# Eight chained layers on one core: quantised weights turned by DMA, feed-forward halves joined, half of attention's queries prepared by GpSimd

## The reference, cut to what matters

```python
x = x + L0_xattn(ln(x), token_ids, ctx, ctx, ctx)   # four experts of 256, silu; a mask by token picks one
x = x + L0_ffn(ln(x), w1, w3, w2)                   # hidden 682, w = clip(round(w/mean|w|), -1, 1) * mean|w|
x = x + L1_wkv(ln(x), ctx, w, u)                    # a recurrence over 256 steps
x = x + L1_moe(ln(x), ...)                          # shared ffn of 352, then 8 fused experts
x = x + L2_attention(ln(x), ctx, ...)               # 16 heads of 16; q, k, v and the probabilities rounded to 8 bits
x = x + L2_ffn(ln(x), w1, w2, w3)                   # hidden 704, w = clip(round(w/mean|w|), -1, 1), sigmoid gate
x = x + L3_linear_attention(ln(x), ctx, ...)
x = x + L3_ffn(ln(x), gate_w, up_w, down_w)         # hidden 1024; x, weights and hidden rounded in blocks of 32 (MX fp8)
```

## Time and profile before

| | us |
|---|---|
| median of 3 runs | 1064.69 (1057.3 to 1065.52) |
| profiled execution, its own time | 1067.97 |
| its span, first to last instruction | 1066.2 |
| PE, DVE, ACT, POOL busy | 874.2 (82%), 737.8 (69%), 459.8 (43%), 147.8 (14%) |
| TensorE clock granted, mean | 0.834 of full |
| chain that ended last | PE 51%, DVE 26%, ACT 9%, issue 7%, DMA 5% |

### The profile page before, as it was taken

How to read it: one execution, slowest core, us unless ns; L and a number is a source line. 1 busy time by engine, 2 the same in 40 slices (tenths; PEclk the granted TensorE clock), 3 DMA queues, 4 the chain that set the end, 5 groups by cost and what they waited for, 6 DMA issues and landing times.

```text
span 1066.2 us, 11685 instructions
## 1 busy us (share of the span) xinstructions
PE 874.2 (82%) x4250; PEld 517.8 (49%) x4250; DVE 737.8 (69%) x968; ACT 459.8 (43%) x694; POOL 147.8 (14%) x230
## 2 busy tenths in 40 slices
PE   5999884489799999988999567777788898878796
PEld 3444562244655555554555233434355566644555
DVE  2774558964457787788487987888864436659773
ACT  2213435642324422222223688989964435422110
POOL 1000000000013443236030111111101000001111
PEclk9999886579989999989999655555559979889898
DMA  8500002100122220330036799877760000000000
GB/s 268 175 0 1 1 0 44 23 3 6 21 44 44 40 36 12 67 51 0 1 45 113 146 152 162 150 138 127 139 93 30 1 0 1 1 0 1 10 10 20
DMA packets 206908, 57.96 MB, mean 54 GB/s; under 512 B 187694, under 2 KB 205188, under 8 KB 206852
## 3 DMA queue, kind: packets, MB, share of 16 engines
q1 hardware_dynamic: 206740, 57.05, 28.4%
q10 hardware_dynamic: 112, 0.17, 0.1%
HBM read 20.62 MB, written 1.05 MB: 20 GB/s over the span
## 4 chain that ended last, share of the span: by engine, by line
PE 51%; DVE 26%; ACT 9%; issue 7%; DMA 5%; POOL 1%; ACTq 1%; POOLq 0%; DVEq 0%
PE ps L900 47%; DMA arena<-xc 4%; DVE arena L2493 3%; ACT xc L1800 3%; ACT arena L1810 1%; PE ps L463 1%; DVE arena L2123 1%; PE ps L1030 1%; DVE xn_t L1940 1%; PE ps L1342 1%; DVE xc L2295 1%; ACT arena_split L1717 1%; DVE arena L2502 1%; DVE sq L2404 1%; DVE sq L2401 1%
## 5 line engine op out<-in xcount | busy, mean ns | idle before, releaser
L900 PE MATMUL ps<-arena 128*128 128x16 f16 (+7 forms) x1760 | 269.4, 324 | 66.5 <-ACT xc L1800 29.9
L900 PE MATMUL ps<-arena_split 128*128 128x512 f32 (+5 forms) x736 | 202.4, 439 | 27.5 <-DVE arena_split L1961 14.6
L900 PEld LDWEIGHTS ps<-arena 128*128 128x128 f16 (+4 forms) x1760 | 133.2, 130 | 177.6 <-issue 82.5
L900 PEld LDWEIGHTS ps<-arena_split 128*128 128x128 f32 (+5 forms) x736 | 136.0, 198 | 99.3 <-issue 39.5
L2493 DVE TENSOR_REDUCE arena<-ps 128x1 f32<-128x1024 f32 x128 | 152.4, 1220 | 28.1 <-PE ps L900 26.4
L1800 ACT ACTIVATE xc<-ps,arena 128x1024 int16<-128x1024 f32 x128 | 153.3, 1203 | 25.2 <-POOL arena L876 20.8
L900 PE MATMUL ps<-sq,arena 128*64 128x256 f32 (+3 forms) x256 | 80.9, 515 | 8.3 <-DVE sq L2404 8.3
L876 POOL TENSOR_SCALAR arena<-arena 128x1 f32<-128x1 f32 x128 | 33.9, 265 | 210.6 <-DVE arena L2493 210.6
L1584 ACT ACTIVATE act_buf<-ps 128x512 f32<-128x512 f32 (+2 forms) x34 | 20.3, 597 | 95.2 <-PE ps L900 95.1
L837 POOL TENSOR_SCALAR arena<-arena 128x512 f32<-128x512 f32 x12 | 23.0, 1921 | 248.3 <-DVE arena L2317 248.3
L900 PEld LDWEIGHTS ps<-sq,arena 128*64 128x64 f32 (+3 forms) x256 | 30.1, 166 | 43.6 <-issue 31.2
(11 more groups left out here) (287 smaller groups left out, 1328.5 us busy)
## 6 DMA issues: line engine op xcount, KB each, us to landing
arena<-in_L_ffn_w SPq DMA_DIRECT2D x4, 640.0 KB, 6.0
arena_split<-arena_split SPq DMA_DIRECT2D x59, 32.0 KB
arena<-xc SPq DMA_TRANSPOSE x96, 3.3
arena<-in_x SPq DMA_DIRECT2D x1, 1024.0 KB, 5.7
arena<-in_ctx SPq DMA_DIRECT2D x1, 1024.0 KB, 8.2
...
```

What stands on the lines that cost most here:

```text
L900: return pe.matmul(o, l, r, start=start, stop=stop)
```

## The change

Six things change. (1) DVE writes the ternary values of both `l0` and `l2` as bf16 into buffers of their own; SP issues the three DMA transposes of `l0` while `l0x` still runs, and ACT copies the result between units 13 and 14 of `l0x`; PE's transposes and GpSimd's casts are gone. (2) In every `ffn` the `down`s of the first half's last units are issued behind the first units of the second half, and `add_y` follows them (`summed`); `ln_steps` for six units becomes earlier in half 0 and later in half 1. (3) DVE makes only the scales of the second half's queries; multiply, rounding and copies are 24 pieces on GpSimd, one behind each of the first 24 row biases; the first half's four copies stand ahead of `xn`. (4) In the last layer the first three steps of `tokens_quantised` stand ahead of the norm's `xc`. (5) The second half of the tokens is quantised in one piece, of which GpSimd does the last three steps. (6) The last tile's gate, product, turn and copy run in two halves of 512 columns, GpSimd rounds the first one, and the last two tiles' `down` use banks 7 and 0.

```diff
-        def ln_steps(n):
+        def ln_steps(n, h):
             if n < 6:
                 return dict(mean=0, xc=0, sq=1, var=1, sd=2, diag=2, rows=2, xn=2, parts=2)
+            if n == 6 and h == 0:
+                return dict(mean=0, xc=0, sq=1, var=1, sd=2, diag=2, rows=3, xn=3, parts=4)
             if n == 6:
-                return dict(mean=1, xc=1, sq=2, var=2, sd=3, diag=3, rows=4, xn=5, parts=5)
+                return dict(mean=2, xc=2, sq=3, var=3, sd=4, diag=4, rows=5, xn=5, parts=5)
...
+            def ternary_turned(name, first):
+                for src, dst, at in zip(ternary_16[name], ternary_back[name], (first, first, first + 1)):
+                    sp.wait_ge(weights_fixed, at)
+                    sp.dma_start_transpose(dst.rearrange("p (a b) -> p a b", b=P), src).then_inc(load[name], 16)
+
+            ternary_turned("l0", 1)
...
+            ternary_turned("l2", 4)
+
             sp.wait_ge(bias_split, 2)
-            for src, dst in zip(ternary_16, ternary_back):
-                sp.dma_start_transpose(dst.rearrange("p (a b) -> p a b", b=P), src).then_inc(load["l2"], 16)
-
-            sp.wait_ge(bias_split, 3)
...
-            pool.wait_ge(weights_fixed, 2)
-            full = H2 // P
-            for w, o in zip(w_l2[0:2], ternary_16[0:2]):
-                o = o.rearrange("p (a b) -> p a b", b=D)
-                step(pool.tensor_copy(o[:, 0:full], w[:, 0:full]))
-                step(pool.tensor_copy(o[0:H2 % P, full], w[0:H2 % P, full]))
-                step(pool.memset(o[H2 % P:P, full], 0.0))
...
+            def late_query(u):
+
+                j, i = divmod(u, 6)
+                if j >= 4:
+                    return
+                if u == 0:
+                    pool.wait_ge(q_scaled, 1)
+                    pool.wait_ge(load["l2"], 16 * 8)
+                v = q_tok[:, 4 + j, :].rearrange("p (h d) -> p h d", d=HD)
+                o = q3[1][:, j]
+                if i == 0:
+                    inv = A["inv"][:, (4 + j) * HEADS:(5 + j) * HEADS]
+                    step(pool.tensor_tensor(v, v, inv.unsqueeze(2).to_broadcast([P, HEADS, HD]), ALU.mult))
+                elif i == 1:
+                    step(pool.tensor_scalar(o[:, :, 0, :], v, ROUND, ROUND, ALU.add, ALU.subtract))
+                else:
+                    n = HEADS // 4
+                    heads = slice(n * (i - 2), n * (i - 1))
+                    last = pool.tensor_copy(o[:, heads, 1:8, :], o[:, heads, 0:1, :].to_broadcast([P, n, 7, HD]))
+                    if i == 5:
+                        last.then_inc(q_split, 1)
...
+                late_query(u)
...
+            def rounded_by(v, power):
+                qf = power.rearrange("p (a b) -> p a b", b=MX_BLOCK)
+                step(pool.tensor_tensor(v, v, qf, ALU.add))
+                step(pool.tensor_tensor(v, v, qf, ALU.subtract))
+
             for t in range(TT):
-                v = h_tok[:, t % 2, :].rearrange("p (a b) -> p a b", b=MX_BLOCK)
+                half = 32 * (t % 2)
+                n = 32 if t < TT - 1 else 16
+                v = h_tok[:, t % 2, 0:n * MX_BLOCK].rearrange("p (a b) -> p a b", b=MX_BLOCK)
+                if t == 2:
+
+                    q = xn_tok[:, 4:8, :].rearrange("p t (a b) -> p (t a) b", b=MX_BLOCK)
+                    pool.wait_ge(xq_ready, 2)
+                    rounded_by(q, mxq[:, 4 * D:8 * D])
+                    back_scaled(q, mx_s[:, 0, 64:96], 32).then_inc(xq_ready, 1)
                 pool.wait_ge(mx_scaled, 24 + t + 1)
-                pool.tensor_tensor(v, v, mx_s[:, 0, 32 * (t % 2):32 * (t % 2) + 32].unsqueeze(2).to_broadcast([P, 32, MX_BLOCK]),
-                                   ALU.mult).then_inc(mx_fixed, 1)
+                if t == TT - 1:
+                    rounded_by(v, mxq[:, 0:n * MX_BLOCK])
+                back_scaled(v, mx_s[:, 0, half:half + n], n).then_inc(mx_fixed, 1)
...
-                        if i >= lag:
-                            down(i - lag)
+
+                        if h * s["n"] + i >= lag:
+                            down(*divmod(h * s["n"] + i - lag, s["n"]))
...
-            pe_turn(pe, "l0")
-            evacuated(pe, marks["l0"][1])
+            pe.wait_ge(weights_fixed, 3)
...
+                    j, c2_ = divmod(n, 2) if t < TT - 1 else (n % 2, n // 2)
...
+            down(TT - 2)
+            last_turned(0)
+            last_turned(1)
+            last_down(0)
+            last_down(1)
...
-            copy_out(act, "l0", False)
+            def ternary_copied(name, wts, h, i):
+
+                full, src, dst = h // P, ternary_back[name][i], wts[i]
+                act.wait_ge(load[name], 16 * 8)
...
+                    v = src.rearrange("p (r k j) -> p k r j", k=KC, j=P)
+                    act.activation(dst[:, :, 0:full * P].rearrange("p k (r j) -> p k r j", j=P), v[:, :, 0:full], ACT.Copy)
+                    act.activation(dst[:, :, full * P:], v[:, :, full, 0:h % P], ACT.Copy)
+
+            def first_ternary(i):
+                for part in {TERN_COPIED: (0, 1), TERN_COPIED + 1: (2,)}.get(i, ()):
+                    ternary_copied("l0", wt_l0, H0, part)
+
+            ffn(l0x, ACT.Silu, between=first_ternary)
             ffn(l0, ACT.Silu, tern_s[0][:, 8:9])
             passed = 0
...
+                def summed(h):
+                    dve.wait_ge(hid_used, s["u0"] + (h + 1) * s["n"])
+                    add_y(h, y_scale).then_inc(x_ready, 1)
...
+                        if h and i == ffn_lag(s) - 1:
+                            summed(h - 1)
...
-                        step(STT(w, w, st[0:r, 12 + i_:13 + i_], t, ALU.is_gt, ALU.subtract))
-                    if i == TERN_SUM + 4:
+                        step(STT(into[j], w, st[0:r, 12 + i_:13 + i_], t, ALU.is_gt, ALU.subtract))
+                    if i in (TERN_SUM + 3, TERN_SUM + 4):
...
-            query_piece(0, 3)
-            query_piece(0, 4)
+            for i in range(3, 7):
+                query_piece(0, i)
             ln_xn_of("l2x", 1)
-            query_piece(0, 5)
-            query_piece(0, 6)
...
-            for i in range(7):
-                query_piece(1, i)
+            query_piece(1, 0)
+            dve.sem_inc(q_scaled, 1)
...
-            ln_xc_of("l3", 1)
...
             dve.wait_ge(xt_copied, 2)
-            tokens_quantised(0, 4).then_inc(xq_ready, 1)
+            tokens_quantised(0, between=lambda: ln_xc_of("l3", 1)).then_inc(xq_ready, 1)
...
+            def last_product(c_):
+                t, one = TT - 1, slice(512 * c_, 512 * c_ + 512)
+                h = h_tok[:, t % 2, one]
+                dve.wait_ge(m_act, TT + c_)
+                dve.wait_ge(m_gu, 2 * TT + 2 * c_)
+                dve.wait_ge(m_ht, t - 1)
+                TTN(h, ps[:, 2 + c_, :], h_act[:, one], ALU.mult).then_inc(m_mul, 1)
+                dve.wait_ge(m_mul, TT + c_)
+                half = slice(32 * (t % 2) + 16 * c_, 32 * (t % 2) + 16 * c_ + 16)
+                mx_quant(h.rearrange("p (a b) -> p a b", b=MX_BLOCK), mxq[:, one], mx_s[:, 0, half], mx_s[:, 1, half], 16,
+                         step, c_ == 1, c_ == 1).then_inc(mx_scaled, 1)
...
-            step(tokens_quantised(4, 2))
+            dve.wait_ge(xq_ready, 1)
+            tokens_quantised(1, rounded=False).then_inc(xq_ready, 1)
             for t in range(TT - 2):
-                product(t + 2)
-                if t == 0:
-                    tokens_quantised(6, 2).then_inc(xq_ready, 1)
-                    dve.wait_ge(xq_ready, 2)
+                if t < TT - 3:
+                    product(t + 2)
+                else:
+                    last_product(0)
+                    last_product(1)
```

199 lines of the change are left out of this document (122 added, 77 removed).

## The result

| | before | changed |
|---|---|---|
| median, us | 1063.64 (1057.3 to 1065.52, 4 runs) | 1029.2 (1027.45 to 1035.36, 4 runs) |
| profiled execution, own time | 1067.97 | 1028.76 |
| span | 1066.2 | 1027.0 |

A forecast was written before the change was run, and what follows sets the result against it. No engine was taken to bound the whole: PE is busy for 82% of the span, with gaps in every stage. Terms summed to -37.4 us, giving 1030.6 from the profiled execution or 1027.3 from the median; forecast 1029, range 1015 to 1042.

The forecast's parts named there:

- Turning, -7.1: Between `l0x` and `l0`: PE's 7.4 us of transposes go, 0.3 for DVE's memsets, DMA transposes and ACT's copies cost nothing.
- The seams, -6.8 and -3.2: Middle of `l0` and `l2`: PE's drain waits go, structure -3.7 and -3.0, the rest clock; longer variance waits counted against.
- a slow stretch behind every variance: Sign in the profile after, at the variances of `l0` and `l2`, that would show the forecast wrong.
- the clock stays as bad: Rival: slow stretches behind all four variance waits, one more in the last layer; 1035 or 1040 us; chance 0.14.
- The casts and attention's start, -0.9 and -4.8: DVE passes no longer slowed beside GpSimd's casts, -0.9; first row maximum 4.8 us earlier at attention's start.
- the seam of `l1`: Middle of `l1`, where DVE's top-six search stays between: 0.3 us gain.
- The pieces, +0.5: Attention's loop: 24 GpSimd pieces between biases, only the rounding longer than the gap, 0.5 us in all; upper bound 12.
- The price of lateness: Attention's loop: each microsecond by which a piece is late costs 24 us; rival at GpSimd's pace 1080, chance 0.02.
- a loop longer than 192 us: Sign in attention's loop that would show the forecast wrong; expected was still 11.9 us for eight units.
- First token pass, second, tail, -1.8, -4.0, -9.0: Last layer: PE's 4.46 wait shrinks 1.8; tile 4's gate starts earlier, -4.0; split last tile ends at 1057.4, -9.0.
- the later of the two ends: Second token pass: `product(2)` ends at 990, not 988.5, if every step with two SBUF inputs waits for GpSimd.
- two sums (1030.6 and 1027.3): Whole kernel: -37.4 taken from the profiled execution, 1067.97, gives 1030.6; from the median, 1064.69, gives 1027.3.

The follow-up runs named there:

- dve_queries: The changed kernel with the second half of the queries on DVE again, ahead of the first row maximum, and no pieces on GpSimd: 1034.95 us, ratio 0.9723.

## Why the prediction was right

- **Turning, -7.1**: 6.0 by the two traces, 6.7 by the mean of ten (98.1), 6.5 by undoing it. Every part of the cover was where it was put.
- **The seams, -6.8 and -3.2**: by undoing them 10.9 for 10.3. The structure was right: the drain's waits are gone, the variance waits 2.24 and 2.15 us (2.4 forecast), `down(6)` waits 0.26 for `add_y` (0.5). The split was not: `l0` gave 5.4 and `l2` 4.5 (means of eight traces). PE's idle time fell by 3.3 us in `l0` (3.7 forecast) and by 3.0 in `l2` (3.0); the rest is clock, 2.1 in `l0` instead of 3.1 and 1.6 in `l2` instead of 0.2. The forecast called a slow stretch behind every variance a sign of being wrong, and three of the four came in each profile of the changed kernel. The rival "the clock stays as bad" had that right (below); it didn't win, since the slow stretches behind the drains, 8.66 and 6.63 us for 20 records, went at the same time.
- **The casts and attention's start, -0.9 and -4.8**: together 5.7, with 0.3 for the seam of `l1` 6.0; measured 5.7 (mean of ten traces). **The pieces, +0.5**: none seen. The price of lateness was taken too high: at twice the length they cost 3.9 by the trace, where a microsecond for each would have given 7. The sign named for it, a loop longer than 192 us, tells nothing: first to last row maximum took 192.0 us before and 193.5 and 191.9 in the two profiles of the changed kernel.
- **First token pass, second, tail, -1.8, -4.0, -9.0**: 14.8, measured 15.3 (mean of eight traces). By undoing it the second pass came out at 2.2 to 4.0, and `product(2)` at 11.6 (10 to 12), the later of the two ends that I gave. The tail came out at 8.6 by undoing it and at 9.5 by the stretch from tile 3 on. Its working has two slips: 1066.2 - 1057.4 is 8.8, not 9.0, and GpSimd's three steps from 1043 end at 1046.6, not 1047.8. Neither mattered, since PE is busy until 1019.5 and GpSimd ends at 1017.0 in the changed kernel. The part of the first pass was not measured by itself.
- Not foreseen: 1.7 us between attention and `l2` (mean of twelve). It is clock: the first eight records of the output projection took 5.38 us before and 3.68 in the changed kernel, while PE's waits in the stage are the same to 0.2 us. `dve_queries`, with the same code there, took 20.53 as the kernel before did.

Undoing the parts gives 6.5 + 10.9 + 5.6 + 2.2 + 8.6 = 33.8 us and the medians fell by 34.4, so that the parts account for the whole within a few microseconds. But in single traces sizes of 2 us are clock and not code. The forecast of 1029 stood between two sums (1030.6 and 1027.3), and the profiled execution fell by 39.2 us where the sum had 37.4. That the median was met to 0.2 us is luck.
